# Moving one 128-byte array from behind the state buffers to in front of them

## The reference, cut to what matters

```
x = x + _L0_conv_ref(_gn(x), ...)     # gate: x * sigmoid(stats of the plane)
x = x + _L1_conv_ref(_gn(x), ...)
x = x + _L2_conv_ref(_gn(x), ...)
x = x + _L3_conv_ref(_gn(x), L3_conv_conv_w, L3_conv_conv_b, L3_conv_prelu_a)

# inside L3: Wc is 1024 x 1024, prev is the column before (4 images, 1024 channels, 32 rows)
def step(prev, x_i):
    y = jnp.einsum('oc,nch->noh', Wc, prev) + conv_b[None, :, None]
    y = jnp.where(y >= 0, y, prelu_a * y)
    cur = y + x_i
    return (cur, cur)
_, fwd_rest = jax.lax.scan(step, x[0], x[1:])
_, bwd_rest = jax.lax.scan(step, fl[-1], fl[:-1], reverse=True)
```

## Time and profile before

| | |
|---|---|
| median of three executions | 854.08 us |
| the profiled execution | 854.0 us |
| its span, first to last instruction | 852.3 us |
| granted TensorE clock over the span | 1.000 of full speed |
| TensorE matmuls busy | 828.0 us, 97% |
| VectorE busy | 660.5 us, 77% |
| ScalarE busy | 421.1 us, 49% |
| GpSimd busy | 66.7 us, 8% |

### The profile page before, as it was taken

How to read it: one execution, slowest core, us unless ns; L and a number is a source line. 1 busy time by engine, 2 the same in 40 slices (tenths; PEclk the granted TensorE clock), 3 DMA queues, 4 the chain that set the end, 5 groups by cost and what they waited for, 6 DMA issues and landing times.

```text
span 852.3 us, 13842 instructions
## 1 busy us (share of the span) xinstructions
PE 828.0 (97%) x4060; PEld 661.3 (78%) x4060; DVE 660.5 (77%) x1461; ACT 421.1 (49%) x1401; POOL 66.7 (8%) x106
## 2 busy tenths in 40 slices
PE   7788899999999999999999999999999999999998
PEld 6743478888888888888888888888888888888887
DVE  6978877777767676676766788888888888888887
ACT  6874455444454445444454444544445444554445
POOL 8963300000000000000000000000000000000000
PEclk9999999999999999999999999999999999999999
DMA  9940200000000000000000023332333223332233
GB/s 381 417 193 0 100 26 0 1 0 0 0 0 0 0 0 0 0 0 0 0 0 0 15 84 98 98 91 62 94 98 98 82 65 98 98 98 73 75 98 99
DMA packets 70654, 56.34 MB, mean 66 GB/s; under 512 B 1904, under 2 KB 66416, under 8 KB 68720
## 3 DMA queue, kind: packets, MB, share of 16 engines
q1 hardware_dynamic: 70640, 56.17, 19.8%
HBM read 39.39 MB, written 16.78 MB: 66 GB/s over the span
## 4 chain that ended last, share of the span: by engine, by line
PE 87%; DVE 4%; DMA 3%; ACT 3%; SPq 1%; issue 1%; DVEq 0%; ACTq 0%
PE ps_prods L706 27%; PE ps_prods L700 26%; PE ps_prods L703 26%; PE ps_turns L722 6%; DMA x_sb<-x_cols 3%; SPq L306 1%; DVE below_flags L1061 1%; ACT stage L541 1%; ACT stage L517 1%; ACT ps_turns L481 1%; DVE cells L1078 0%; ACT w_hi L512 0%; PE ps_values L652 0%; ACT ps_prods L481 0%; PE ps_group L663 0%
## 5 line engine op out<-in xcount | busy, mean ns | idle before, releaser
L700 PE MATMUL ps_prods<-w_hi,s_hi 128*128 128x512 f32 x990 | 397.1, 401 | 0.0
L703 PE MATMUL ps_prods<-w_lo,s_hi 128*128 128x512 f32 x990 | 394.7, 399 | 0.0
L706 PE MATMUL ps_prods<-w_hi,s_lo 128*128 128x512 f32 x990 | 387.6, 392 | 0.0
L551 ACT ACTIVATE act_buf<-ps_prods 128x256 f32<-128x256 f32 x247 | 81.8, 383 | 338.1 <-PE ps_prods L706 333.0
L1167 DVE SCALAR_TENSOR_TENSOR x_sb<-act_buf,x_sb 128x256 f32 (+1 forms) x247 | 105.1, 426 | 143.7 <-ACT act_buf L558 133.7
L706 PEld LDWEIGHTS ps_prods<-w_hi,s_lo 128*128 128x128 f32 x990 | 186.4, 188 | 35.6
L700 PEld LDWEIGHTS ps_prods<-w_hi,s_hi 128*128 128x128 f32 x990 | 186.1, 188 | 33.5
L703 PEld LDWEIGHTS ps_prods<-w_lo,s_hi 128*128 128x128 f32 x990 | 186.5, 188 | 31.1
L558 ACT ACTIVATE act_buf<-ps_turns,bias 128x128 f32<-128x128 f32 x494 | 156.7, 376 | 49.5 <-PE ps_turns L722 49.5
L564 ACT ACTIVATE ps_below<-ps_turns,neg_bias 128x128 f32<-128x128 f32 x494 | 152.1, 361 | 0.0
L1174 DVE SCALAR_TENSOR_TENSOR x_sb<-ps_below,neg_slope,x_sb 128x256 f32 (+1 forms) x247 | 118.8, 481 | 5.4
(11 more groups left out here) (208 smaller groups left out, 369.2 us busy)
## 6 DMA issues: line engine op xcount, KB each, us to landing
stage<-x_cols SPq DMA_DIRECT2D x31, 512.0 KB, 3.9
out_cols<-x_sb SPq DMA_DIRECT2D x31, 512.0 KB, 4.6
x_sb<-x_cols SPq DMA_DIRECT2D x15, 1024.0 KB, 18.5
w_raw<-w_t SPq DMA_DIRECT2D x8, 512.0 KB, 19.1
x_sb<-x_cols SPq DMA_DIRECT2D x1, 2048.0 KB, 8.0
x_sb<-x_cols SPq DMA_DIRECT2D x2, 512.0 KB, 27.3
out_cols<-x_sb SPq DMA_DIRECT2D x4, 128.0 KB, 2.1
params<-gates SPq DMA_DIRECT2D x1, 60.0 KB, 14.2
```

The source lines that it names most:

```text
L551: act.activation(act_buf[:, half], ps_prod[c if bank is None else bank][:, half], ACT.Copy) .then_inc(raw_copied, 1)
L700: pe.matmul(out, s_hi[:, k, :], w_hi[:, k, w_cols], start=(k == 0), stop=False)
L703: pe.matmul(out, s_hi[:, k, :], w_lo[:, k, w_cols], start=False, stop=False)
L706: return pe.matmul(out, s_lo[:, k, :], w_hi[:, k, w_cols], start=False, stop=(k == CT - 1))
```

## The change

The declaration of `both_scale` moves from behind `act_buf` to in front of the arrays of `tmp`, outside of what `scratch.close()` gives up.

```
--- before
+++ after
@@ -95,6 +95,7 @@
         sloped_bias = sb("sloped_bias", [P, 2])
 
 
+        both_scale = sb("both_scale", [P, N, CT])
         scratch = ExitStack()
 
         def tmp(name, shape, dt=fp32):
@@ -152,7 +153,6 @@
         s_hi = sb("s_hi", [P, CT, NH], fp32r)
         s_lo = sb("s_lo", [P, CT, NH], fp32r)
         act_buf = sb("act_buf", [P, HALF])
-        both_scale = sb("both_scale", [P, N, CT])
         both_shift = sb("both_shift", [P, N, CT])
 
         spreading = ExitStack()
```

## The result

The changed kernel takes 864.36 us (median of 4, 864.14 to 864.55), the kernel before, on the same chips, 854.12 us. The ratio is 1.0119, with a 95% interval of 1.0107 to 1.0132. The forecast was 854.1 us with a range to 857.0: the kernel became 10.2 us slower where no change was expected.

A forecast was written before the change was run, and what follows sets the result against it. The prediction took TensorE's matmul pace to bound the scan, 85% of the span. Every term of the address change was put at 0, leaving the forecast at 854.1 us, with a range of 852.0 to 857.0.

The forecast's parts named there:

- no change: Whole kernel: a time between 852.4 and 855.8 us, a change below 0.2%, 1.7 us; chance 0.75.
- the term for the pace of the stream at the new distance: Scan matmuls: distance 320 between states and weights leaves the pace unchanged; taken as 0, bounds 11.8 us on both sides.
- What bounds the kernel: Scan, 85% of the span: bound by how fast TensorE takes matmuls, with other engines inside their slack.
- The pace is thus 97% the moving operand: Scan matmuls of 512 columns: 0.2288 us each, of which only 0.007 us is fixed whatever the width.
- Three offsets, one duration: TensorE's stationary loads: 188 to 189 ns from three address offsets, so 188 at the new one; term 0.
- Distance 0 and distance 192 have one pace: Warm-ups at 0.233 us against restart matmuls at 0.232: distance from stationary to moving array makes no difference.
- The pace goes the other way: Slower rival, scan: load and stream collide at distance 320 but not 192; up to 11.8 us, 865.9 us; chance 0.08.
- The bound that I had worked out, 11.8 us on both sides: Scan stream pace: 4 ns for each of 2952 products, kept as the limit of the term taken as 0.
- The rival of VectorE's reads: Slower, scan: colliding reads in lines 1167 and 1142 make the low state late; 42 us, 896 us; chance 0.06.
- The faster rival: Scan: load takes 4.6 ns from each product and the new offset cures it; 13.6 us, 840.5 us; chance 0.11.
- The argument from the read ports: TensorE: independent read ports for moving operand and LDWEIGHTS, so load and stream don't meet and nothing needs curing.

The follow-up runs named there:

- e13: Kernel before, but the scan's products stream the first weight column of each block, repeated, so the stream stays on one address; 815.13 us.
- e14: Changed kernel's addresses, but the scan's products stream the first weight column of each block, repeated; 814.78 us.
- e5: Kernel before with a gap in front of s_hi, states and turn buffer 64 bytes higher, small arrays of the statistics staying; 850.9 us.

## Why the prediction was wrong

The step that failed is the term for the pace of the stream at the new distance, which I put at 0. It measured about 4 ns for each product, 10.2 us. Two readings had led to the 0, and both were wrong: that the pace is nearly all moving operand, and that distances 0 and 192 have one pace.

**What bounds the kernel: right.** TensorE's pace bounds the scan, and the whole difference is pace. The first product starts 0.06 us later than before, and 4.5 ns on 2952 matmuls would be 13.3 us; 10.1 came. Compared start by start over the two traces from the first transposes on, the 2720 distances from one product to the next grew by 4.0 ns on average, 10.8 us in all; the second and third behind a pair of transposes grew least. The 247 from a product to the transposes that follow shrank by 0.6 us together.

**"The pace is thus 97% the moving operand": wrong, and the root of it.** I had split the pace into a part for each column and one for each matmul, from two widths, and found 7 ns that a load could cost. After the change the same working gives 0.2333 - 2 x (0.2333 - 0.1147) = -0.004 us for a matmul, which can't be. So a matmul of 512 columns doesn't cost what two of 256 do, and two widths can't be split this way; why the two widths went opposite ways isn't shown. The excess over 0.216 us was 13 ns, and all of it went when the stream stood still (e13). The number was in the rows: bf16 fillers at 0.2157 against 0.2288. I took only the difference of the two fixed parts from it, 4.6 ns.

**"Three offsets, one duration": true and beside the point.** The loads stay between 188 and 190 ns at every placement, in e13 and e14 as well. The duration of a load says nothing of what it does to the stream, so these rows could not carry the term of 0.

**"Distance 0 and distance 192 have one pace": wrong.** Settled, they have 0.2265 (e5) and 0.2288 us. I compared eight warm-ups with five matmuls behind a restart, and neither stands for the settled pace. In e5, at distance 0 like the warm-ups, matmuls behind transposes take 0.237 us in the step shown and settled ones 0.2265. Why the five at distance 192 took 0.232 isn't shown; they also come in the other order of the first step. And of the distance that the change makes, 320, I had no row at all.

**The rivals.** "The pace goes the other way" is what happened: 4.5 ns where I bounded it by 4, 864.4 us where I priced 865.9. It was named, and its mechanism, its place in the scan and its size were right; it had 0.08, while no change had 0.75. The bound that I had worked out, 11.8 us on both sides, was then left outside of the range. The rival of VectorE's reads fell: lines 1142 and 1167 have 426 ns as before. The faster rival named the same cause, and a third of its size: 38 us went with the walk, not 13.6, though the best of eight placements gives back 3.5.

**The argument from the read ports.** I let the Trainium skill, "SBUF — State Buffer", section "Who interferes with whom", speak against a meeting of load and stream: it gives TensorE two independent read ports, and says that this engine never waits on anyone. The measurements decide otherwise for this kernel: the same loads and streams take 850.9, 854.1 or 867.0 us by distance alone, and 815 when the stream stands still. What that section says of VectorE and GpSimd no run here tests: VectorE's operations in the scan kept their durations, and GpSimd has no instruction there.

**What stays open.** That the loads of the states and the stream of the weights get in each other's way, by the distance between them, is shown; what they meet in is not. A part of the memory that both want at once, repeating every 256 bytes, would fit, but no run looked inside. Why 192 and 0 are good and 224 between them is not, and why the rhythm has a period of two after and of three before, isn't explained either. A stream at rest also asks less of the memory in other ways than by not meeting the load. No run keeps the walk and takes the loads away, so how much of the 13 ns a walking float32r stream would cost by itself is open. The bf16 fillers don't settle it: they walk as well, at 0.2157 us, but over half the bytes for each column, and the same 128 columns four times. What e14 shows is that the placement no longer matters once the stream stands still.

## What to carry to other kernels

Where float32r matmuls follow each other closely and each has its own load, the place of the stationary array against the moving one is a parameter, here worth 16 us of 850 between best and worst. An edit that adds or moves a small array changes it unseen, so two versions should be compared at equal distances, or a few gaps of 32 to 224 bytes should be tried on each. A pace above that of a bf16 filler of the same width (0.2288 against 0.2157 us here) is the sign to look for.

## What the runs showed of the hardware

- Float32r matmuls of 512 columns with one 128 x 128 load each start 0.2265 (e5), 0.2288 (before) or 0.2333 us (after) apart by placement, and 0.2158 us apart when the moving operand is one repeated column.
- The dependence on the distance between the two repeated after 256 bytes where that was tried (states 0, 256 and 512 bytes up: 854.1 to 854.2 us; 128 and 384: 864.4 and 865.3), is not smooth on steps of 32 bytes (854.1, 864.0, 850.9, 865.1), and leaves the loads' own 188 to 190 ns unchanged.
- The placement that is better for 512 columns was the worse one for 256, in the one stretch of these: 0.2288 and 0.1179 us before, 0.2333 and 0.1147 after.
